# The last stage of a fused vision block: tile steps in a new order, with part of the next turn's first layer done a turn ahead

## What is computed

```python
logits = xn2 @ w_gate
top_vals, top_idx = jax.lax.top_k(logits, 2)
gates = jax.nn.softmax(top_vals, axis=-1)
gates_full = zeros((T, E)).at[arange(T)[:, None], top_idx].add(gates)
def body(acc, p):
    w1, bb1, w2, bb2, g = p
    h = jax.nn.gelu(xn2 @ w1 + bb1, approximate=False)
    return (acc + g[:, None] * (h @ w2 + bb2), None)
```

## Time and profile before

| | |
|---|---|
| median of 3 runs | 2629.07 us (2626.32 to 2637.59) |
| profiled execution | 2648.85 us, span of its instructions 2647.0 us |
| busy in the span | PE 90%, PE weight loads 69%, DVE 63%, ACT 44%, POOL 39% |
| stage of tiles alone | from 2182 us of the span to its end |

### The profile page before, as it was taken

The page is one execution under the profiler, slowest core; times in us unless marked ns, Lnnn a source line. Parts: engine busy times, 40 slices in busy tenths (PEclk is TensorE's granted clock), DMA queues, the critical chain, the costliest instruction groups (busy, mean ns, idle before and its releaser), DMA issues. The chain is left out here.

```text
span 2647.0 us, 64056 instructions
## 1 busy us (share of the span) xinstructions
PE 2375.2 (90%) x19496; PEld 1831.0 (69%) x19496; DVE 1658.9 (63%) x4146; ACT 1158.1 (44%) x2240; POOL 1041.5 (39%) x1196
## 2 busy tenths in 40 slices
PE   5489999899999999889999999999999878988896
PEld 3356666666666666677777777777777657978886
DVE  3358888888888888866767776677776631111111
ACT  2133444334443444345555555555555523333332
POOL 2013333333333323243444444444444334555555
PEclk8669999999999999899999999999999988999998
DMA  6423222231222222544444445545453336877875
GB/s 135 113 54 50 32 31 35 42 47 31 35 32 48 40 31 35 133 87 96 104 108 104 104 104 116 116 108 107 93 114 99 98 100 207 208 218 207 216 208 127
DMA packets 250836, 262.98 MB, mean 99 GB/s; under 512 B 35476, under 2 KB 230488, under 8 KB 250776
## 3 DMA queue, kind: packets, MB, share of 16 engines
q1 hardware_dynamic: 213912, 229.95, 36.7%
q0 software_dynamic: 36864, 32.27, 7.0%
HBM read 212.21 MB, written 52.83 MB: 100 GB/s over the span
## 5 line engine op out<-in xcount | busy, mean ns | idle before, releaser
L820 POOL DMA_INDIRECT out<-big,tokn x192 | 304.1, 1584 | 475.0 <-DVE big L1427 258.3
L1277 DVE TENSOR_REDUCE MX<-PS 108x2 f32<-108x648 f32 x576 | 456.0, 824 | 43.5 <-PE PS L1699 37.9
L972 ACT ACTIVATE pool<-PS 108x648 f32<-108x648 f32 x576 | 387.2, 713 | 210.2 <-PE PS L1722 178.8
L1578 PE MATMUL PS<-WB,big 128*128 128x192 f32 x2304 | 406.6, 332 | 3.4 <-ACT big L1001 3.4
L1001 ACT ACTIVATE big<-PS,WF 128x256 f32<-128x256 f32 x576 | 241.8, 472 | 371.1 <-PE PS L1578 327.6
L1578 PE MATMUL PS<-XE,WF 128*128 128x256 f16 x2880 | 366.5, 279 | 41.4 <-DMA WF<-w1p 29.1
L1578 PEld LDWEIGHTS PS<-WB,big 128*128 128x128 f32 x2304 | 375.3, 192 | 27.3 <-issue 17.1
L1578 PEld LDWEIGHTS PS<-XE,WF 128*128 128x128 f16 x2880 | 276.9, 100 | 98.8 <-issue 33.9
L797 POOL DMA_INDIRECT xbuf<-XR,DST x192 | 190.4, 992 | 230.4 <-issue 168.8
L1427 DVE SCALAR_TENSOR_TENSOR big<-PS,grow,GB 128x192 f32<-128x192 f32 x192 | 71.3, 413 | 287.8 <-POOL GB L808 148.4
L1699 PE MATMUL PS<-KH,QA 32*108 32x324 f16 x1152 | 158.6, 338 | 62.7 <-ACT Vp L957 21.0
(11 more groups left out here) (197 smaller groups left out, 4090.3 us busy)
## 6 DMA issues: line engine op xcount, KB each, us to landing
WF<-w1p SPq DMA_DIRECT2D x96, 771.5 KB, 7.0
WB<-in_L_ffn_W SPq DMA_DIRECT2D x96, 576.0 KB
ximg<-in_x SPq DMA_DIRECT2D x96, 196.0 KB, 5.5
XtR<-xbuf SPq DMA_DIRECT2D x96, 196.0 KB
ximg<-in_x SPq DMA_DIRECT2D x96, 195.1 KB, 8.7
B2t<-in_L_ffn_b SPq DMA_DIRECT2D x96, 96.0 KB
out<-R SPq DMA_DIRECT2D x32, 243.0 KB
w1p<-WF SPq DMA_DIRECT2D x8, 768.0 KB, 4.4
```

Source lines behind the costliest of these rows:

```text
L820: nc.gpsimd.indirect_dma_start(rows_out, bass.IndirectOffsetOnAxis(ap=tokn[:, i, s_:s_ + 1], axis=0), Yt[:, i, s_, :], None, bounds_check= ...
L972: nc.scalar.activation(Pr[:, at:at + 2, :], pair(("st", p))[0:TP, :, 0:T], ACT.Exp, scale=SCALE2).then_inc(S["ex"], 1)
L1277: nc.vector.tensor_reduce(MX[:, qt, g, 64 * jj:64 * jj + 64:32], pair(("s", p))[0:TP, :, 0:T], AX.X, ALU.max).then_inc(S["mx"], 1)
L1578: last = nc.tensor.matmul(out_ap, lhsT, rhs, start=(i == 0), stop=(i == len(products) - 1))
```

## The change

`TILE_STEPS` has the same steps in another order, and the `ahead` list grows from (X 0, xe 0) to (X 0, xe 0, W1 0 0, ge 0 0, W1 0 1, ge 0 1, X 1, xe 1). The three `W2` steps, which stood at the places 22, 42 and 47 of the list, are now a third of a turn apart. The steps that are done ahead are issued once before the first turn of the stage. No arithmetic changes. PSUM banks are given out anew for `X`.

```diff
 TILE_STEPS = [
-    ("gm", 0), ("gb", 0), ("lr", 0), ("W1", 0, 0), ("ge", 0, 0), ("X", 1), ("xe", 1), ("gm", 1), ("gb", 1), ("lr", 1),
...
+    ("gm", 0), ("gb", 0), ("lr", 0), ("W1", 0, 2), ("ge", 0, 2), ("lu", 0), ("gm", 1), ("gb", 1), ("lr", 1),
...
 ]
-ATTEND, BOTH, TILES = Plan(ATTEND_STEPS, ATTEND_BANKS), Plan(BOTH_STEPS, BOTH_BANKS), Plan(TILE_STEPS, TILE_BANKS, (("X", 0), ("xe", 0)))
+ATTEND, BOTH, TILES = Plan(ATTEND_STEPS, ATTEND_BANKS), Plan(BOTH_STEPS, BOTH_BANKS), Plan(TILE_STEPS, TILE_BANKS, (("X", 0), ("xe", 0), ("W1", 0, 0), ("ge", 0, 0), ("W1", 0, 1), ("ge", 0, 1), ("X", 1), ("xe", 1)))
@@ ScalarE, before the first turn
             xe(B + 2 - LAG, 0)
+            ge(B + 2 - LAG, 0, 0)
+            ge(B + 2 - LAG, 0, 1)
+            xe(B + 2 - LAG, 1)
@@ TensorE, before the first turn
-            x_turn(Turn(TILES, None, None, None, B + 1 - LAG), B + 2 - LAG, 0)
+            first, turn = B + 2 - LAG, Turn(TILES, None, None, None, B + 1 - LAG)
+            x_turn(turn, first, 0)
+            w1_unit(turn, first, 0, 0)
+            w1_unit(turn, first, 0, 1)
+            x_turn(turn, first, 1)
```

## The result

The changed kernel takes 2643.15 us, median of 11 runs (2633.84 to 2651.04). The kernel before takes 2629.58 us in the same comparison (2625.03 to 2640.50, 11 runs). The ratio is 1.0056, 95% interval 1.0037 to 1.0074: 13.6 us slower, where 22.5 us faster was forecast. Against the bound of 0.5% the middle is just a loss, and the interval reaches down to 0.4%. That the time rose is clear of the noise.

The account below looks back on a forecast made before the run. The prediction took the unbroken chain of adds as the bound; -1.6 + 0.3 - 0.2 = -1.5 us a turn, over 15 turns -22.5, gave 2629.07 - 22.5 = 2606.6, rounded to 2607 us, range 2588 to 2634.

Parts of the forecast that it names:

- The chain of adds bounds the stage: Last stage: POOL's adds form one unbroken chain of 26.12 us a turn, while PE needs only 22.54.
- Even spacing of W2 is worth nothing: On PE, spacing W2 evenly gains 0 us by itself, since results already wait for the chain.
- WF of tile 0 goes out beside add 1, and add 2 gains 1.6 us: On SP, the load goes out 5.4 us sooner, leaving add 2: -1.6 us a turn, bounds -1.8 and 0.
- Add 1 loses 0.3: Add 1 shares its time with the moved WF load: +0.3 us a turn, bounds 0 and +2.3.
- The swap of WB and WF gains add 0 0.2: Add 0 meets a WF and a WB load, not two WF: -0.2 us a turn, bounds 0 and -2.0.
- Sum: Per turn of the last stage: -1.6 + 0.3 - 0.2 = -1.5 us, over 15 turns -22.5 us.
- start and end: First turn and last three adds of the stage: counted 0 us; the start is bounded by -2 and +3.
- Contention only changes its place: Rival: add 1 loses the 1.6 us that add 2 gains; turn stays 26.1, time 2629 us; chance 0.22.
- The slower rival: WF of tile 0 still in flight at add 2: add 1 pays 1.5 us a turn, 2652 us; chance 0.12.
- add 1 went over 9 us: Sign that the steps are wrong: add 1 in the last stage takes over 9 us.
- A wait of POOL for DVE: Sign that the steps are wrong: POOL waits for DVE in place of landings.
- PE did not idle 22 us less: Sign expected if the steps are right: PE idles about 22 us less in the stretch.

Follow-up runs that it names:

- e7: Kernel before with the chain cut: adds wait only for the same tile's previous add, into three separate buffers, results missing from output; 2592.29 us, ratio 0.9810.
- e8: Changed kernel with the chain cut: adds wait only for the same tile's previous add, into three separate buffers, results missing from output; 2593.48 us, ratio 0.9809.
- e3: Changed kernel with SP's order of before put back in full, keeping the new order on PE and ACT; 2632.81 us, ratio 0.9981.
- e5: Changed kernel whose WF load of tile 0 brings only its last 7 columns in the stage of tiles alone; 2632.79 us, ratio 0.9948.
- e4: Changed kernel with only the WF load of tile 2 put back ahead of the WB load of tile 1; 2651.29 us, ratio 1.0052.
- e12: e10 with the WB load of tile 0 held behind the rows of tile 2 on SP; 2632.98 us, ratio 0.9991 to the kernel before.
- e10: Changed kernel with gb 0 computed a turn ahead on POOL, behind add 1 and ahead of add 2; 2654.24 us, ratio 1.0065.
- e6: Changed kernel with gb 1 moved behind add 0 on POOL, leaving two GB pieces between add 2 and the next add; 2653.11 us, ratio 1.0037.
- e9: Kernel before whose WF load of tile 0 brings only its last 7 columns in the stage of tiles alone; 2627.80 us, ratio 0.9953.
- e1: Changed kernel with only the WF load of tile 0 put back behind the rows of tile 1 on SP; 2632.68 us, ratio 0.9990.
- e2: Kernel before with SP's order of the changed kernel, PE and ACT as before; 2656.41 us, ratio 1.0075.

## Why the prediction was wrong, step by step

- **The chain of adds bounds the stage.** Right. Cutting it gave 1.9% and a stage bound by PE at the 22.54 us of the prediction (e7, e8). Even spacing of W2 is worth nothing: nearly right, 0.2% with the chain (e3) and nothing without it (e8).
- **WF of tile 0 goes out beside add 1, and add 2 gains 1.6 us.** Right: 1.55 us behind the rows load, and add 2 from 8.57 to 7.06, -1.5.
- **Add 1 loses 0.3.** This step failed. It lost 1.6 (8.27 to 9.88). I had said that "an add beside one WF load takes about 8.1" and took the difference to add 1's mean, as if the load came in place of the burst that add 1 meets. It comes on top of it: e5 has the burst without the load at 8.10, the same as before's 8.27, and the load adds 1.8. The prediction's upper bound for this term, +2.3 from the adds beside two WF loads, held it.
- **The swap of WB and WF gains add 0 0.2.** The swap is worth nothing (e4). But add 0 rose by 0.6 (9.30 to 9.93), which the prediction had no term for. In the table add 0 is 9.8 to 10.1 in each kernel whose add 2 is 7.1 or less, and 9.0 to 9.5 in each whose add 2 is 8.5 or more. The WB load of tile 0 goes out at a fixed time behind the issue of add 2, so the sooner add 0 starts, the more of that load it should meet. That cause I have only argued. In the change it lands on average 0.2 us before the end of add 0's issue, in the kernel before some 1.9 us before it, as far as its landings are on record. In e12 it goes out 2.1 us into add 0, so it is beside that add as well, and add 0 takes 9.94.
- **Sum.** +0.6 + 1.6 - 1.5 = +0.7 us a turn in place of -1.5; times 15 that is +10.3 us, and +0.5 at start and end: 10.8 of the 13.6 us between the medians. The rest is within the spread of the runs.
- **The rivals.** "Contention only changes its place" is what the loads did: 13.13 us of landing a turn before, 13.19 after. The rule that I weighed against my sum, in the Trainium skill, "DMA: Bandwidth & Descriptors", section "Issuing engines are not separate DMA queues", agrees with these sums, though e10 (14.66 us with the same loads) shows that the sum is not fixed for every order. But that rival forecast no change, 2629 us, and it left out, as I did, that a wait under a floor is free. Add 2 has a floor of 6.8 us. The prediction named it as 6.4 and put it down to POOL's four pieces alone; e6 shows that yv 0 holds it as long without two of them. A load beside add 2 costs its landing 2.4 us and the chain 1.0; the same load beside add 1 costs 1.8 and the chain 1.6. The change took the load from the only add that had slack. The slower rival, WF still in flight at add 2, had add 1 pay 1.5 us, which is nearly what it paid, but tied that to an add 2 that stays long. Add 2 became short, in all turns from 17 on.
- **The signs.** Of the prediction's signs of being wrong one came: add 1 went over 9 us. A wait of POOL for DVE came in the guise of "issue". PE did not idle 22 us less, but 1.3 us more.
- **The gap in the reasoning** was to credit add 2 with the whole load and to debit add 1 with a mean. The near constancy of adds 0 and 1 together, which stood in the prediction as the rival's argument, should have been given the price of the load on both sides: -1.6 and +1.6, and then nothing is left to gain.

None of the versions tried with all their work beats the kernel before by 0.5%; e3 comes nearest, 0.2%. The chain itself is worth 1.9%. Whether adds of different experts' tiles, or adds to different rows, can be let go without the wait was not tried.

## What to carry to other kernels

When a transfer is moved from beside one link of a serial chain to beside another, debit the new link with the full price that the old one is credited with, and ask which of the links has a second, parallel way round that makes a delay free: a load belongs beside the link whose floor hides it. A step that is taken off a floor should be checked for its other readers, for what it releases may fall on the same link (e10). And comparing two profiled executions of one change should start at the last common row, since here the unchanged part differed by 13.7 us.

## What the runs showed of the hardware

- An accumulating add of two times 128 rows lands 1.2 us after its issue with nothing beside it, on average 1.8 to 2.0 us beside one small rows load, and 3.5 to 5.8 us beside weight loads (table). One transfer of 771.5 KB cost it 1.8 us (e5) and 2.4 us (e9). So over a turn most of the landing time, 13.1 us where three adds alone would land in 3.6, is other queues' traffic.
- The same bytes in another order changed the DMA share from 0.81 to 0.74 (e1, e2), and the better order was the one that put a load where the chain would else have waited for compute.
- With the chain cut, the DMA share rose to 0.91 and 0.94 at 246 and 245 GB/s (e7, e8), so 0.80 at 214 was not a limit of the DMA engines.
- From the end of DVE's yv 0 to the start of the add that reads it on POOL it is 0.96 us, and from the landing of an add to the next one's start 0.85; three such steps and the issue of the transfers, 12.9 us, are half of every turn of 26.
